# Attention in a four-part kernel: another order of projections, row transfers, the opening and the row statistics

## The reference

```python
x = x + attn(layernorm(x))          # x: (4 sequences, 1024 rows, 256)
Q, K, V = (multilora(x, ids, W, A, B) for each of q, k, v)   # base + low rank
Q, K = rope(Q), rope(K)             # 16 heads of 16
scores = where(causal, Q @ K.T / 4, -inf)
out = multilora(softmax(scores) @ V, ids, Wo, Ao, Bo)
```

## Time and profile before

| what | us |
|---|---|
| median of 3 runs (2184.39, 2202.07, 2201.05) | 2201.05 |
| profiled execution, its own time | 2185.0 |
| its span | 2183.1 |
| opening, to the first exponential | 131.4 |
| the 16 units | 131.4 to 790.7 |
| attention's end, start of the feed-forward layer's work | 819.8 |
| PE, DVE, ACT, POOL busy over the span | 1819.3, 1191.3, 822.7, 725.6 |

### The profile page before, as it was taken

The page is one execution under the profiler, slowest core; times in us unless marked ns, Lnnn a source line. Parts: engine busy times, 40 slices in busy tenths (PEclk is TensorE's granted clock), DMA queues, the critical chain, the costliest instruction groups (busy, mean ns, idle before and its releaser), DMA issues. The chain is left out here.

```text
span 2183.1 us, 30159 instructions
## 1 busy us (share of the span) xinstructions
PE 1819.3 (83%) x9520; PEld 1212.1 (56%) x9520; DVE 1191.3 (55%) x2979; ACT 822.7 (38%) x1705; POOL 725.6 (33%) x922
## 2 busy tenths in 40 slices
PE   5368889889888864899999658989898938999997
PEld 3133334434433322788888535747484727888886
DVE  4466676666666508543443356665656685443442
ACT  2036655656665624111111035554646441111111
POOL 2335464464462312222222124333242312222221
PEclk9569989989988855999999969999999978999999
DMA  5522333332442108000000230100101080000000
GB/s 160 174 89 90 119 126 95 122 125 77 134 135 87 39 16 313 22 24 28 26 25 26 70 111 15 43 36 1 78 1 78 1 309 22 26 24 30 25 24 9
DMA packets 90179, 161.23 MB, mean 74 GB/s; under 512 B 23080, under 2 KB 50476, under 8 KB 88880
## 3 DMA queue, kind: packets, MB, share of 16 engines
q1 hardware_dynamic: 71504, 107.39, 14.7%
q0 software_dynamic: 17984, 50.62, 7.2%
q10 hardware_dynamic: 544, 1.31, 0.2%
HBM read 102.52 MB, written 45.48 MB: 68 GB/s over the span
## 5 line engine op out<-in xcount | busy, mean ns | idle before, releaser
L690 ACT ACTIVATE a_probs<-a_ps_e 128x512 f32<-128x512 f32 (+3 forms) x768 | 336.0, 491 | 204.1 <-PE a_ps_e L854 200.9
L438 DVE CUSTOM_DVE_ANT_0 a_ps_m<-a_ps_m,a_causal 128x512 f32<-128x512 f32 (+3 forms) x512 | 239.4, 517 | 97.5 <-PE a_ps_m L841 96.4
L1433 PE MATMUL g_ps_y<-g_w_d,x_res 128*128 x1120 | 253.2, 379 | 2.8 <-DVE x_res L1203 2.8
L854 PE MATMUL a_ps_e<-a_q_st,a_k_st 64*128 64x512 f32 (+3 forms) x768 | 187.9, 480 | 76.4 <-ACT a_probs L690 48.5
L854 PEld LDWEIGHTS a_ps_e<-a_q_st,a_k_st 64*128 64x128 f32 x768 | 79.6, 201 | 289.8 <-ACT a_probs L690 200.5
L1433 PEld LDWEIGHTS g_ps_y<-g_w_d,x_res 128*128 128x128 f32 x1120 | 212.3, 190 | 34.6 <-issue 3.2
L442 DVE TENSOR_REDUCE a_peak<-a_ps_m 128x1 f32<-128x512 f32 x256 | 164.8, 686 | 94.8 <-PE a_ps_m L841 94.1
L841 PE MATMUL a_ps_m<-a_k_st,a_q_st 64*128 64x512 f32 (+3 forms) x768 | 152.7, 399 | 68.8 <-DMA a_k_st<-a_scr_k 28.0
L1323 ACT COPY x_res<-g_ps_h 128x512 f32<-128x512 f32 x70 | 41.1, 587 | 439.2 <-PE g_ps_h L1441 439.2
L576 POOL TENSOR_SCALAR_AFFINE_SELECT a_probs<-a_probs 128x256 f32<-128x256 f32 x256 | 103.9, 408 | 284.1 <-ACT a_probs L690 283.8
L1170 DVE BATCH_NORM_STATS2 g_xe_stats<-x_res 128x6 f32<-128x256 f32 x70 | 29.9, 426 | 295.6 <-DMA x_res<-g_x_rows,g_token_i 295.6
(11 more groups left out here) (272 smaller groups left out, 3664.5 us busy)
## 6 DMA issues: line engine op xcount, KB each, us to landing
a_q_st<-a_scr_q POOLq DMA_DIRECT2D x32, 512.0 KB, 4.0
a_k_st<-a_scr_k POOLq DMA_DIRECT2D x32, 512.0 KB, 4.8
m_spread_acs<-m_acs_rows SPq DMA_DIRECT2D x8, 2048.0 KB, 9.7
a_scr_q<-a_high SPq DMA_DIRECT2D x36, 256.0 KB
a_scr_k<-a_high SPq DMA_DIRECT2D x36, 256.0 KB
a_swapped<-a_raw SPq DMA_DIRECT2D x64, 128.0 KB, 2.0
g_w_gu<-L_ffn_Wg SPq DMA_DIRECT2D x8, 1024.0 KB, 9.8
g_w_gu<-L_ffn_Wu SPq DMA_DIRECT2D x8, 1024.0 KB, 12.4
```

Source lines behind the costliest of these rows:

```text
L438: nc.vector.tensor_tensor_reduce(ps_m[:, bank, 0:w], ps_m[:, bank, 0:w], causal[:, 512 - w:], 1.0, MASKED, ALU.add, ALU.max, peak[:, p % 2 ...
L690: nc.scalar.activation(probs[:, N % RING, r, q0:], ps_e[:, (2 * N + r) % HEAD_BANKS, q0:], ACT.Exp, scale=DH ** -0.5).then_inc(exp_done, 1)
L854: nc.tensor.matmul(ps_e[:, (2 * N + r) % HEAD_BANKS, q0:], k_st[rows(r), p % BUFS, j * P:(j + 1) * P], q_st[rows(r), p % BUFS, 512 * c + q ...
L1433: last = nc.tensor.matmul(ps_y[:, 0:D], hid_t[:, f * P:(f + 1) * P], w_d[:, bass.ds(e, 1), f].rearrange("p a d -> p (a d)"), start=(f == 0 ...
```

## The change

- `QK_AT` and `V_AT` go from steps 3, 5, 7, 9 to 2, 8, 14, 20; `LORA_O_AT` from 13 to 11. SP's swaps stand at steps 3, 9, 15, 21, its keeps at 11, 17, 23 and 5 of the unit after. POOL's rope goes to steps 5 to 7, 11 to 13, 17 to 19, and 23, 0 and 1 of the unit after. ACT's `round_high` goes to steps 8, 14, 20 and 2 of the unit after.
- `put_rows` goes from POOL to SP, at the step of the turn itself; a `bitcast` leaves no conversion to the transfer, and ACT writes `less_t` rounded.
- In the opening projections 2 and 3 of block 0 have own buffers in the free space of `probs`; ACT issues the keeps of 1 and 3; SP waits for the first pair before it loads X; the order of SP's keeps, rows and swaps is another.
- Statistics of sequence 1 go between chunks 22 to 42, those of 2 and 3 into units 1 and 5 (steps 10 to 17, and 20).

```diff
@@ -140,7 +140,7 @@
-    LORA_AT, XT_AT, OUT_AT, QK_AT, V_AT, LORA_O_AT = (1, 4, 9), (6, 7, 12, 13), (15, 17, 19, 21), (3, 5, 7, 9), (3, 5, 7, 9), 13
+    LORA_AT, XT_AT, OUT_AT, QK_AT, V_AT, LORA_O_AT = (1, 4, 9), (6, 7, 12, 13), (15, 17, 19, 21), (2, 8, 14, 20), (2, 8, 14, 20), 11
@@ -204,6 +204,8 @@
         spare = probs[:].rearrange("p r h q -> p (r h q)")
+        first_high = spare[:, 2560:3584].rearrange("p (n q) -> p n q", n=2)
+        first_low = spare[:, 3584:4608].rearrange("p (n q) -> p n q", n=2)
         w_nat = spare[:, 0:2048].rearrange("p (m t d) -> p m t d", m=4, t=2)
@@ -268,6 +270,20 @@
+        def parts(blk, i):
+            if blk == 0 and i >= 2:
+                return first_high[:, i % 2], first_low[:, i % 2]
+            return high[:, i % 2], low[:, i % 2]
+        def keep(eng, blk, i):
+            eng.wait_ge(low_ready, 4 * blk + i + 1)
+            n, half = i % 2, i // 2
+            to = scr[n][blk % 2, :, :, :, half * 512:(half + 1) * 512]
+            hi, lo = parts(blk, i)
+            for c, part in enumerate(((hi, hi, None, lo), (hi, lo, None, hi))[n]):
+                if part is not None:
+                    eng.dma_start(to[:, c], part).then_inc(scr_out[i % 2], 16)
         block = ctx.enter_context(nc.Block())
@@ -296,14 +312,11 @@
-            def keep(blk, i):
...
+            def put_rows(p):
+                sp.wait_ge(piece_act, ACT_NO["max", p] + 1)
+                for r in range(2):
+                    sp.dma_start(q_st[64 * r + 32:64 * r + 33, p % BUFS, :].bitcast(F32), less_t[r * T:(r + 1) * T, p % 2, :]).then_inc(rows_in[p % BUFS], 16)
@@ -340,18 +353,26 @@
                 swap(0, i)
-            for i in range(4):
-                keep(0, i)
+            for i in (0, 2):
+                keep(sp, 0, i)
+            sp.wait_ge(pair_in[0], 32)
             for b in range(1, BATCH):
                 sp.dma_start(X[:, b * T:(b + 1) * T], x[:, b * T:(b + 1) * T]).then_inc(x_in[b], 16)
-            for i in range(4):
+            for i in range(3):
                 swap(1, i)
-            for i in range(4):
-                keep(1, i)
+            keep(sp, 1, 0)
+            put_rows(0)
+            swap(1, 3)
+            for i in (1, 2):
+                keep(sp, 1, i)
+            put_rows(1)
+            keep(sp, 1, 3)
             for U in range(UNITS):
...
                 for n in range(CORE):
+                    for p in MAX_AT.get(U * CORE + n, []):
+                        put_rows(p)
                     if U >= 1 and n == 2:
@@ -360,12 +381,12 @@
                         spread_inverse(U // 2 - 1, 1)
-                    if g % 2 == 1 and more and n in (4, 6, 8, 11):
-                        swap(2 * b + 2 + g // 2, (4, 6, 8, 11).index(n))
-                    if g % 2 == 1 and more and n in (17, 19):
-                        keep(2 * b + 2 + g // 2, (17, 19).index(n))
-                    if g % 2 == 0 and U >= 2 and (U - 1) // GROUPS + 1 < BATCH and n in (3, 6):
-                        keep((U - 1) // GROUPS * 2 + 2 + (U - 1) % GROUPS // 2, 2 + (3, 6).index(n))
+                    if g % 2 == 1 and more and n in (3, 9, 15, 21):
+                        swap(2 * b + 2 + g // 2, (3, 9, 15, 21).index(n))
+                    if g % 2 == 1 and more and n in (11, 17, 23):
+                        keep(sp, 2 * b + 2 + g // 2, (11, 17, 23).index(n))
+                    if g % 2 == 0 and U >= 2 and (U - 1) // GROUPS + 1 < BATCH and n == 5:
+                        keep(sp, (U - 1) // GROUPS * 2 + 2 + (U - 1) % GROUPS // 2, 3)
                     if n == (22 if g == 0 else 11):
@@ -396,9 +417,13 @@
+            def row_moments(b, t):
+                if t == 0:
+                    dve.wait_ge(x_in[b], 32 if b == 0 else 16)
+                step(nc.vector.bn_stats(stats[:, b * T + t], X[:, b * T + t]), wait=False)
             def moments(b):
-                for t in range(b * T, (b + 1) * T):
-                    step(nc.vector.bn_stats(stats[:, t], X[:, t]), wait=t + 1 == (b + 1) * T)
+                dve.wait_ge(dve_step, step.n)
                 for t in range(b * T, (b + 1) * T):
@@ -467,7 +492,8 @@
-            dve.wait_ge(x_in[0], 32)
+            for t in range(T):
+                row_moments(0, t)
             moments(0)
@@ -481,10 +507,12 @@
                     merge(0, 3)
-            for b in range(1, BATCH):
-                dve.wait_ge(x_in[b], 16)
-                moments(b)
-            maxima(0, CUTS[0])
+            for k in range(0, CUTS[0], 2):
+                maxima(k, k + 2)
+                if k in range(22, 22 + 2 * T, 2):
+                    row_moments(1, (k - 22) // 2)
+                if k == 42:
+                    moments(1)
             for U in range(UNITS):
@@ -501,6 +529,10 @@
                         norm(b + 1, t + 1)
+                    if g == 1 and b + 2 < BATCH and n in range(10, 10 + T):
+                        row_moments(b + 2, n - 10)
+                    if g == 1 and b + 2 < BATCH and n == 20:
+                        moments(b + 2)
                     if U % 2 == 1 and n == 17:
@@ -543,7 +575,8 @@
                 pool.wait_ge(high_ready, 4 * blk + i + 1)
-                nc.gpsimd.tensor_tensor(low[:, i % 2], raw[:, i], high[:, i % 2], ALU.subtract).then_inc(low_ready, 1)
+                hi, lo = parts(blk, i)
+                nc.gpsimd.tensor_tensor(lo, raw[:, i], hi, ALU.subtract).then_inc(low_ready, 1)
@@ -559,14 +592,6 @@
-            def put_rows(p):
-                pool.wait_ge(piece_act, ACT_NO["max", p] + 1)
-                pool.wait_ge(chunk_max, (p + 1) * NC)
...
             def mask(U, n):
@@ -591,8 +616,6 @@
                 load(p)
-            for b in range(1, BATCH):
-                inverse_std(b)
             pool.wait_ge(rope_in, 16)
@@ -601,13 +624,12 @@
                     remainder(1, i - 1)
-                if i == 2:
-                    put_rows(0)
+            inverse_std(1)
             remainder(1, 3)
-            put_rows(1)
-            ROPE_AT = {6: (0, 0), 7: (0, 1), 8: (0, 2), 9: (1, 0), 10: (1, 1), 11: (1, 2), 12: (2, 0), 13: (2, 1),
-                       14: (2, 2), 15: (0, 3), 17: (1, 3), 19: (3, 0), 21: (3, 1), 23: (3, 2)}
+            ROPE_AT = {5: (0, 0), 6: (0, 1), 7: (0, 2), 9: (0, 3), 11: (1, 0), 12: (1, 1), 13: (1, 2), 15: (1, 3),
+                       17: (2, 0), 18: (2, 1), 19: (2, 2), 21: (2, 3), 23: (3, 0)}
+            ROPE_THEN = {0: 1, 1: 2, 3: 3}
             for U in range(UNITS):
@@ -620,17 +642,21 @@
                             remainder(2 * b + 2 + g // 2, i)
-                    if g % 2 == 0 and U >= 2 and (U - 1) // GROUPS + 1 < BATCH and n in (1, 4):
-                        remainder((U - 1) // GROUPS * 2 + 2 + (U - 1) % GROUPS // 2, 2 + (1, 4).index(n))
+                    if g % 2 == 0 and U >= 2 and (U - 1) // GROUPS + 1 < BATCH and n in ROPE_THEN:
+                        blk, part = (U - 1) // GROUPS * 2 + 2 + (U - 1) % GROUPS // 2, ROPE_THEN[n]
+                        if part < 3:
+                            rotate(blk, 3, part)
+                        else:
+                            remainder(blk, 3)
                     if n == 0 and U >= 1 and U + 1 < UNITS:
...
                         load(2 * (U + 2))
-                    for p in MAX_AT.get(U * CORE + n - 1, []):
-                        put_rows(p)
+                    if g == 1 and b + 2 < BATCH and n == 22:
+                        inverse_std(b + 2)
                     if g == 3 and b + 2 < BATCH and n in (10, 11, 12):
                         select(b + 2, n - 10)
-                    if g == 2 and b >= 1 and n == 9:
+                    if g == 2 and b >= 1 and n == 8:
                         select(b, 3)
@@ -663,15 +689,15 @@
                         act.wait_ge(rows_in[(k - 2) % BUFS], 32 * ((k - 2) // BUFS + 1))
-                    nc.scalar.copy(less_t[:, k % 2], bank[0:2 * T, 0:P]).then_inc(piece_act, 1)
+                    nc.scalar.copy(less_t[:, k % 2].bitcast(F32R), bank[0:2 * T, 0:P]).then_inc(piece_act, 1)
...
                     act.wait_ge(scr_filled, 16 * 8)
-                if blk >= 1 or i >= 2:
+                if blk >= 1:
                     act.wait_ge(scr_out[i % 2], 48 * (2 * blk + i // 2))
-                nc.scalar.copy(high[:, i % 2].bitcast(F32R), raw[:, i]).then_inc(high_ready, 1)
+                nc.scalar.copy(parts(blk, i)[0].bitcast(F32R), raw[:, i]).then_inc(high_ready, 1)
@@ -705,6 +731,8 @@
                         round_high(0, i)
+                    for i in (1, 3):
+                        keep(act, 0, i)
                 if e in ACT_NO:
@@ -724,8 +752,8 @@
                         take_sums(U, 0)
-                    if g % 2 == 1 and more and n in (11, 14, 21):
-                        round_high(2 * b + 2 + g // 2, (11, 14, 21).index(n))
+                    if g % 2 == 1 and more and n in (8, 14, 20):
+                        round_high(2 * b + 2 + g // 2, (8, 14, 20).index(n))
```

9 lines of the change are left out of this document (removed).

## The result

| | before | after |
|---|---|---|
| median of the runs side by side | 2200.89 us | 2219.68 us |
| ratio | 1 | 1.0107, interval 1.0064 to 1.0150 |
| profiled execution: span | 2183.1 us | 2218.0 us |
| second step's exponential | 140.26 us | 120.43 us |
| end of attention | 791.0 us | 827.9 us |

The account below looks back on a forecast made before the run. No single engine was taken to bound attention. From 2185.0: - 27.0 opening - 13.7 rows - 5.6 loads + 12.3 and 12.0 new waits + 7.8 places + 3.8 statistics = 2174.6; half the gap between run levels gave 2183, range 2150 to 2206.

Parts of the forecast that it names:

- The opening: Before the units: own buffers, earlier loads and moved statistics bring unit 0's second step 27.0 us earlier; bounds 12 and 31.
- ACT issues six transfers at 0.6 each: Opening: after rounding until 50.4, ACT's issues end at 54.3 in place of 60.8, so loads come at 60.0.
- The rival that block 1's rope is held: Opening held by transfers: block 1's rope holds ACT before unit 0, the gain is 12, time 2198; chance 0.14.
- can't land before X: Opening: block 1's swaps, behind X on SP's queue, land after it; 21 in place of 27 if all delay counted.
- Rows: Rows through SP: all of TensorE's 13.7 us of waits in six units goes; bounds 0 and 13.7.
- The wait in odd units: ACT's exponential of step 9 waits behind rounding for POOL's rope: 2.1 us in six units, 12.3; bounds 0 and 18.
- The rival that the rope is in time: 2 us less anywhere in take_sums, collect, swap, rope removes half of the two new waits: 2159; chance 0.24.
- The wait in even units: ACT's rounding waits for POOL's rope: 3.0 us in units 4, 8, 12, 1.0 in 2, 6, 10; 12.0 together.
- Places: Projections at the new steps cost 7.3 us against 6.0: plus 1.3 in six units, 7.8; nothing for V.
- The rival that spreading hides the projections: TensorE's short idle pieces take 2 us more per unit in nine units: 2157; chance 0.10.
- The statistics: Those of two sequences, at steps 10 to 17 of units 1 and 5, cost 1.9 us each, 3.8; bounds 0 and 7.
- 38 in the rival: Slower by the clock: twelve new waits for six that go, 3.2 us each through half clock, 2221; chance 0.10.

Follow-up runs that it names:

- e7: The kernel before with the rows of maxima alone issued by SyncE, not by GpSimd; ratio 0.9967.
- e5: The changed kernel with the unit schedule of before, and POOL's scaling of a pair's first half at step 8 of the even unit; ratio 0.9770.
- e2: The changed kernel with SP's first swap of an odd unit ahead of the five transfers of collect; ratio 0.9951.
- e12: The changed kernel, places spread, with POOL's scaling at step 8 of the even unit and each block's first swap ahead of the sums' transfers; ratio 0.9923.
- e3: The changed kernel with the schedule inside the units put back to that of before; ratio 0.9894.
- e11: The kernel before with ScalarE held by eight idle copies at step 8 of six odd units; ratio 1.0179, 2231.4 us.
- e13: e11 with TensorE's wait behind the copies filled with 14 matmuls that nothing reads; ratio 1.0072, 2209.9 us.
- e14: The changed kernel with 20 idle matmuls in each of its twelve new waits; ratio 0.9915.
- e6: The changed kernel with 12 idle matmuls in each of its twelve new waits; ratio 1.0046.
- e17: e15 with 12 idle matmuls at step 4 of the even units 2 to 12; ratio 0.9758, 2140.9 us.
- e16: e5 unchanged, run again beside e15 on the same chip; ratio 0.9790, 2148.3 us.
- e15: e5 with all four parts of the first block kept by SyncE, none by ScalarE; ratio 0.9771.

## Why the prediction was wrong, point by point

- **The opening: 27.0 forecast, 19.8 measured.** First maximum at 71.8, not 66.3: the step "ACT issues six transfers at 0.6 each" failed. The 0.6 came from one transfer of the sums; here they took 1.5. The trace of the kernel before had it, in SP's first stores of key parts, with nobody else storing:

```profile
46.34 1.35 SPq L306 DMA_DIRECT2D a_scr_k<-a_high  x1
47.73 1.56 SPq L306 DMA_DIRECT2D a_scr_k<-a_low  x1
49.33 1.68 SPq L306 DMA_DIRECT2D a_scr_k<-a_high  x1
```

The load at 65.58 came 0.8 before that of the earlier trace rows, not 6. The gain is from what stood behind it: X is loaded after the first pair, so scores start 5.4 us after the load's issue and not 9.1, which is 4.5 of the 16.7 us that the first maximum gained, and DVE isn't at statistics then, which is the rest. The rest of the wait for the row was 1.82, forecast 1.7. The rival that block 1's rope is held did not occur. Against e7 the opening is worth 0.7%, 16 us. Block 1's first swap stands behind X on SP's queue, and the rope can start 8.9 us after its issue, not 2.66. The Trainium skill ("DMA: Bandwidth & Descriptors", section "Queues, rings and completion order") has each DMA engine consume descriptors in ring order, and lets a later one finish its write before an earlier one. The timeline agrees: the first of the swap's two transfers landed at 88.5, shortly before the last of X at 89.0, so my "can't land before X" was too strong. By the rows the delay cost nothing, as I had chosen: DVE is busy 21.81 of the last 23.90 us of the opening, and its maxima set the end.

```profile
80.84 13.91 SPq L313 DMA_DIRECT2D a_swapped<-a_raw  x6
...
89.74 1.26 POOL L568 TENSOR_TENSOR a_raw<-a_raw,a_rope 128x512 f32<-128x512 f32 x1 [17.85 <-DMA a_swapped<-a_raw]
```

```profile
93.70:117.60 23.90, 14.04 (x42) 6.23 (x40) 21.81 (x70) 3.40 (x8) 17.65 (x14) 0.57 0.37 114
```

- **Rows: 13.7 forecast, and 5.6 for the loads; 7 measured for both (interval -1 to 16).** The waits for rows are gone; the step that failed is "all of it". POOL's wait for the reciprocals and ACT's for the stored part stood behind them at the same time and came out. Only e5 has the reciprocals' wait gone too. The two stalls for loads went nearly as forecast: units 3 and 7 fall from 40.5 and 40.4 to 38.1 in e7, 4.7 of 5.6.
- **The wait in odd units: 2.1 each forecast, 2.87 in unit 5.** The six are 2.5 to 4.1 long, 17.9 in all against 12.3. Place, chain and releaser were right. The rope ended within 0.3 us of where the sum puts it after unit 5's start; ACT was ready 1.0 us sooner than in the sum, and waited that much longer. The rival that the rope is in time did not occur; its own price was off as well, since it lets half of the waits go and takes all 24 us off.
- **The wait in even units: right for 4, 8 and 12, wrong for 2, 6 and 10.** Forecast 1.0 for these, but units 2 and 6 have 3.25: POOL still has the inverse root and the scaling ahead of the rope's second part, and the scaling ends 4.3 us into unit 6, not at 2.4. Unit 10, which has no inverse root, has 1.56. All twelve waits sum to 35.4 against 24.3, 11 us too little. POOL and ACT in unit 6 of after, which starts at 396.5:

```profile
396.36 1.67 POOL L90 TENSOR_TENSOR a_rstd<-a_var_eps,table 128x8 f32<-128x8 f32 x1
...
399.62 1.25 POOL L608 TENSOR_TENSOR a_out_t<-a_out_t,a_den 128x512 f32<-128x512 f32 x1
...
403.98 1.27 POOL L574 TENSOR_TENSOR a_raw<-a_raw,a_swapped 128x512 f32<-128x512 f32 x1
...
405.28 0.62 ACT L700 CAST a_high<-a_raw 128x512 fp32r<-128x512 f32 x1 [3.25 <-POOL a_raw L574]
```

- **Places: 1.3 in an odd unit forecast, about 2.0 measured** (39.6 in units 1 and 3 of e2, with the wait mended and at full clock, against 37.6 to 37.7 in units 1 and 9 before). The rival that spreading hides the projections did not occur: e12 loses to e5. The statistics, forecast at 3.8, cost nothing: units 1 and 5 take 37.8 and 37.6 in e3.
- **The clock: nothing in the sum, 38 in the rival; some 23 of the 35 us between the two profiles.** The step that failed is the term put at nothing on the ground that the clock comes back soon. Units 1 to 14 took 624.3 with the waits idle and 586.0 with them filled, 38 us apart with 137 us less half clock: 0.28 us for each. The change added 81 us of half clock (125 to 206), so its share is 23 us, an estimate. 34 of the 81 lie in units 13 and 14, where no new wait is and where it comes and goes from profile to profile. The clocks of all runs, over which such chance averages out, say less: a mean granted clock of 0.895 in the 90 runs of the kernel before that stand beside the experiments, and 0.886 in the five of the kernel after. That is 47 us more half clock, or 13 of the 25 us between the means. So by the profiles the clock is the largest single term that I missed, but it doesn't decide the sign by itself: without its share the kernel would stand some 12 us, half a percent, over the one before, at the edge of what the interval can tell from no change. The profile missed my sum, 2174.6, by 45 us. Clock 23, waits 11, opening 7 and rows and loads some 12 (19.3 forecast, 7 measured) are 53, so these shares are rough.
- **Why I put it at nothing.** I argued from means: "units 2 and 3 have a mean of 0.96". But the waits for rows left TensorE idle 1.8 to 2.9 us, and mine leave it idle 2.8 to 4.7; I never worked out TensorE's idle time, only ACT's. Nor did I use the only number at hand for the size I was making, unit 12's 9.5 us, in the sum. The rival's price was right, 3.2 us per wait against 3.1 in e11 and e13, and its chance of 0.10 was too low. That its total fits so well (2221 against 2219.7) is luck: it charges all twelve waits and credits nothing for the six that go, though the even units had 82 us of half clock before and have 82 after. What it charges too much makes up for the terms above that were too good. That e14's units come out 16.6 over before, which is my sum for the units, is luck too.

## What to carry to other kernels

When an edit makes an in-order engine wait, work out how long TensorE then stands still, not only how late the next result is: here six waits of 0.9 us moved the time by 0.2%, and six of 3.5 us cost 3.1 us more each through the clock. If such a wait can't be avoided, fill it with matmuls into a free bank; that is also the cleanest test of whether the clock is to blame, if the kernel before is filled as well, which wasn't done here. Fill it whole, and only where half clock follows: e6 and e17 show what else happens. And before a wait is priced at its own length, look which other engines wait in the same microseconds: their waits take its place, and the gain only comes when both go.

## What the runs showed of the hardware

- The granted clock fell in all six units behind 3.5 us in which TensorE was idle, and in none of the six when that time was filled; after 0.92 us it fell in three of six, later in the unit. In unit 5 of e11 it stayed at 0.50 for at least 7 us although TensorE was busy for 6.70 of 7.01 us; in the six units half clock came to 7 to 14 us each.
- How long it stays down isn't set by the kernel alone. e5 and e16 are the same kernel: unit 13 had 3.3 us of half clock in one profile and 17.0 in the other. In the kernel after, units 13 and 14 had 17 each with no new wait in them. Why the clock stays low there is open.
- An issue of a stored part held ACT for 1.6 us on average (e16). SP, which in e15 issues all twelve, took 0.6 to 0.7 for each of the first three and 1.2 to 1.6 for each of the others. What lengthens them is open: in e16 SP's last store is issued by 51.05, and three of ACT's, begun at 54.49, still take 1.6 each, so that both engines issue at the same time is not the reason.
- DVE's two small operations on the maxima, of 128x8 and 128x16, took 1.26 and 1.20 us in the opening of the kernel after and 0.17 each before. They stood beside POOL's operations of 1.26 and 1.27 that began at 89.74 and 90.96, and ended with them. The same pair stretches again at 109.5 and 110.8, beside POOL. The Trainium skill ("GPSIMD Engine Reference", section "1. Specifications") says that the two engines share their way to SBUF, with contention for DVE's instructions in a two-port mode or with two inputs in SBUF. The first of the two has two inputs, and its time agrees with that; the second has one, and no run here shows which mode it ran in.

```profile
89.76 1.26 DVE L475 TENSOR_TENSOR a_peak<-a_peak 128x8 f32<-128x8 f32 x1
91.06 1.20 DVE L478 TENSOR_SCALAR a_less<-a_peak 128x16 f32<-128x16 f32 x1
```
